# A compressed-interaction layer in pairs of chunks over two PSUM banks

## The reference

```python
# input: (512, 64, 16); W0: (128, 64*64); W1, W2: (128, 64*128)
for W, b in params:
    z = jnp.einsum('bhd,bfd->bhfd', x_vec, input)
    B, h, f, d = z.shape
    z = z.reshape(B, h * f, d)
    x_vec = jnp.einsum('oc,bcd->bod', W, z) + b[None, :, None]
    outs.append(x_vec.sum(axis=2))
return jnp.concatenate(outs, axis=1)
```

## Time and profile before

| | us |
|---|---|
| median of 3 runs | 1128.33 |
| lowest, highest | 1128.06, 1129.62 |
| the profiled execution | 1127.95 |
| its span, first to last instruction | 1126.2 |
| TensorE busy | 1095.7 |
| VectorE busy | 868.8 |
| GpSimd busy | 836.8 |
| ScalarE busy | 451.4 |

### The profile page before, as it was taken

How to read it: one execution, slowest core, us unless ns; L and a number is a source line. 1 busy time by engine, 2 the same in 40 slices (tenths; PEclk the granted TensorE clock), 3 DMA queues, 4 the chain that set the end, 5 groups by cost and what they waited for, 6 DMA issues and landing times.

```text
span 1126.2 us, 17047 instructions
## 1 busy us (share of the span) xinstructions
PE 1095.7 (97%) x4690; PEld 786.3 (70%) x4690; DVE 868.8 (77%) x3008; ACT 451.4 (40%) x1533; POOL 836.8 (74%) x765
## 2 busy tenths in 40 slices
PE   5989999999999999999999999999999999999996
PEld 5766667666677667666678666676677776666776
DVE  3556879888884888879794798978887598888990
ACT  1443435343432444434351343534343243434550
POOL 4568887969784697878875788787978479697561
PEclk9999999999999999999999999999999999999998
DMA  7952414223141231405141051423323142240000
GB/s 245 251 114 60 112 54 94 73 56 104 17 122 36 58 102 24 124 27 122 46 103 47 17 122 45 105 62 80 87 42 95 31 94 73 51 109 9 1 1 29
DMA packets 112352, 85.82 MB, mean 76 GB/s; under 512 B 75136, under 2 KB 77920, under 8 KB 112128
## 3 DMA queue, kind: packets, MB, share of 16 engines
q1 hardware_dynamic: 110528, 78.37, 28.9%
q10 hardware_dynamic: 1728, 6.36, 1.5%
HBM read 14.75 MB, written 0.79 MB: 14 GB/s over the span
## 4 chain that ended last, share of the span: by engine, by line
PE 83%; DVE 13%; issue 2%; DMA 1%; ACT 1%; POOL 1%; SPq 0%; POOLq 0%; ACTq 0%
PE y L692 53%; PE l L705 19%; DVE acc L619 8%; PE xt L755 5%; PE l2p L767 3%; DVE bd L584 2%; DVE w1l L673 1%; DVE x1l L594 1%; DMA gram<-in_L_rec_W_dram 1%; PE l2p L744 1%; DMA z<-xg 0%; PE l2p L717 0%; ACT prod L525 0%; PE xt L737 0%; PE l L727 0%
## 5 line engine op out<-in xcount | busy, mean ns | idle before, releaser
L619 DVE SCALAR_TENSOR_TENSOR acc<-y,x0t,acc 128x128 f32<-128x128 f32 x2560 | 698.8, 341 | 206.1 <-PE y L692 204.0
L525 ACT ACTIVATE prod<-y,x0t 128x128 f32<-128x128 f32 x1280 | 366.0, 369 | 610.5 <-PE y L692 578.7
L692 PE MATMUL y<-w1h,x1h 128*128 128x512 f32 x1024 | 509.3, 497 | 6.0 <-DVE acc L619 4.3
L692 PE MATMUL y<-w1h,x1l 128*128 128x512 f32 x1024 | 403.5, 394 | 0.0
L692 PE MATMUL y<-w1l,x1h 128*128 128x512 f32 x1024 | 402.4, 393 | 0.0
L371 POOL TENSOR_TENSOR pacc<-pacc,prod 128x512 f32<-128x512 f32 x192 | 247.4, 1289 | 191.6 <-ACT prod L525 191.6
L360 POOL TENSOR_TENSOR z<-z,xg 128x512 f32<-128x512 f32 (+2 forms) x272 | 348.3, 1288 | 23.7 <-DMA z<-xg 23.7
L692 PEld LDWEIGHTS y<-w1h,x1h 128*128 128x128 f32 x1024 | 192.8, 188 | 132.8 <-issue 59.2
L705 PE MATMUL l<-z,w0t 128*128 128x512 f32 (+1 forms) x512 | 257.5, 585 | 0.6 <-POOL z L360 0.6
L692 PEld LDWEIGHTS y<-w1l,x1h 128*128 128x128 f32 x1024 | 192.8, 188 | 82.2 <-issue 54.1
L692 PEld LDWEIGHTS y<-w1h,x1l 128*128 128x128 f32 x1024 | 192.1, 188 | 43.6
(11 more groups left out here) (65 smaller groups left out, 300.8 us busy)
## 6 DMA issues: line engine op xcount, KB each, us to landing
z<-xg SPq DMA_DIRECT2D x480, 128.0 KB, 2.4
xg<-in_r_input_dram SPq DMA_DIRECT2D x32, 128.0 KB, 3.9
w2t<-in_L_rec_W_dram ACTq DMA_DIRECT2D x8, 512.0 KB, 7.1
gram<-in_L_rec_W_dram SPq DMA_DIRECT2D x8, 512.0 KB, 5.9
z<-xg SPq DMA_DIRECT2D x32, 96.0 KB, 4.0
z<-xg SPq DMA_DIRECT2D x15, 192.0 KB
gram<-in_L_rec_W_dram ACTq DMA_DIRECT2D x1, 2048.0 KB, 7.9
out_dram<-z SPq DMA_DIRECT2D x4, 192.0 KB, 2.1
```

What stands on the lines that cost most here:

```text
L525: last = nc.scalar.activation(prod[:, h % HSLOTS, k, :], y[c % YB][:, k * O:(k + 1) * O], ACT.Copy, scale=x0t[:, j, f:f + 1])
L619: ins = nc.vector.scalar_tensor_tensor(out=to, in0=of, scalar=x0t[:, j, f:f + 1], in1=b1r[:] if m == 0 else to, op0=ALU.mult, op1=ALU.add)
L692: ins = nc.tensor.matmul(to, stationary, moving, start=(first and k == 0), stop=(last and k == 2))
```

## The change

`chunk` is replaced by `two_chunks`, which runs at even c for the chunks c and c + 1. The wait for the bank is split off as `bank_free`. For each of the two chunks it waits for the bank and does the two passes with x1h; then come the two passes with x1l, each of which completes a chunk and raises `y_made`. So x1h is the stationary operand of four passes in a row and x1l of two, and two banks are open at once. The number of passes and the arithmetic per bank are as before, and the other engines' lists are the same.

```diff
-            def chunk(tile, j, c):
+            def bank_free(tile, c):
 
                 before, late = (c - YB) % CHUNKS, c < YB
                 if before in HELPED:
@@ -777,9 +777,17 @@
                 else:
                     value = SN * tile + (SN + CF * SUMMED.index(before) + CF) - (SN if late else 0)
                     pe.wait_ge(acc_step, value)
+
+            def two_chunks(tile, j, c):
+
                 cols = slice(j * P, (j + 1) * P)
-                by_parts(y[c % YB][:], x1h[:, cols], x1l[:, cols], w1h[:, c, :], w1l[:, c, :],
-                         True, True, True).then_inc(y_made, 1)
+                for k in (c, c + 1):
+                    bank_free(tile, k)
+                    nc.tensor.matmul(y[k % YB][:], x1h[:, cols], w1h[:, k, :], start=True, stop=False)
+                    nc.tensor.matmul(y[k % YB][:], x1h[:, cols], w1l[:, k, :], start=False, stop=False)
+                for k in (c, c + 1):
+                    nc.tensor.matmul(y[k % YB][:], x1l[:, cols], w1h[:, k, :], start=False,
+                                     stop=True).then_inc(y_made, 1)
...
-                    chunk(tile, j, c)
+                    if c % 2 == 0:
+                        two_chunks(tile, j, c)
```

## The result

The changed kernel takes 1143.64 us (median of 4, 1142.66 to 1144.25) against 1128.19 for the kernel before in the same comparison: a ratio of 1.0135, interval 1.0123 to 1.0147. It is 15.5 us slower; 1142 was forecast.

The account below looks back on a forecast made before the run. TensorE was taken to bound most of a group, VectorE a dense stretch around each group's end. 1127.95 + 11.7 + 3.0 - 1.0 = 1141.7, with 0.4 to the median 1142 us; range 1129 to 1150, about 0.8.

Parts of the forecast that it names:

- Part 1, the loads: TensorE's weight loads: 4690 as before, all hidden; steps with changed or unchanged operand give -3 to +3 us, -1 taken.
- holding pays: Rival, chance 0.12: TensorE steps keeping their operand cost 0.213 us, saving 16 us in all, so 1126.
- Part 2, the passage: Dense stretch, chunks 56 to 9' (stroke: next group): later results and bank stalls, 0.78 us per group, +11.7 us over fifteen.
- The last group: Group without layer 0, VectorE-paced: tiles go from 12.10 to 13.07 us; three remaining tiles add +3.0 us.
- What else moves: Layer-0 steps, layer-2 matmuls and W2 turns now behind odd chunks: counted as nothing, -1 to +1 us.
- The slip at 56 is absorbed: Rival, chance 0.14: the 0.42 us at chunk 56 is lost, waits at 61, 3', 7' stay; 1136.
- Nothing changes: Rival, chance 0.08: the four banks cushion everything and loads are as before; 1128.
- it spreads: Rival, chance 0.06: each of the 48 tiles with layer 0 also stalls one step, 11 us more; 1153.

Follow-up runs that it names:

- snake: Changed kernel's pairs with one bank open at a time, second chunk starting with its x1l pass so operands are still held; 1125.4 us, beside 1125.0 for moved.
- moved: Changed kernel's pairs with passes chunk by chunk, so only layer-0, layer-2 and turn work due at even chunks moves behind the odd chunk; 1125.0 us.
- own_moved: moved, with bd for a group's last tile made on VectorE after chunk 50 instead of 59; 1115.3 us.

## Why the prediction was right, and where it was off

- **Part 1, the loads: right, but its -1 us was not there.** 4690 loads, all behind passes but those held back by a wait; `snake` shows that holding gives nothing (1125.4 to 1125.0), so the term is 0. The rival "holding pays" is out. The rule of the Trainium skill that I set against the trace (TensorE: Matmul & The Clock Gate, section The mechanism) fails again: the changed kernel and `snake` load the same rows behind streaming passes and keep 0.23 a step.
- **Part 2, the passage: right in place and size.** Stalls forecast at 61, 0', 3', 4', 7' as 0.44, 0.58, 0.17, 0.11, 0.33; measured 0.45, 0.47, 0.16, 0.12, 0.33. The shift of VectorE's chain was 0.47 for 0.42. Against the kernel before, a group got 0.69 longer for the forecast 0.78, and 0.81 longer against `moved`: the 0.11 of the moved work lies between. The two halves, tried alone, and VectorE's load, taken away, show the mechanism and not only its sum.
- **The last group: right in kind, small by a fifth.** Tiles 13.27 apart for 13.07, so the term of 3.0 us was nearer 3.9 (from chunk 56 of the fifteenth group to the end of VectorE's work +4.6, less 0.7 for the passage). VectorE waits at 8 and 14 as said: by the distance of starts 2, 6, 8 and 14 come 0.11, 0.12, 0.35 and 0.35 late, for 0.1, 0.1, 0.35 and 0.45. The missing 0.2 is bd: from chunk 11's first operation to chunk 12's are 1.99 us for 1.76, with bd itself at 1.03 instead of 0.81. It is longer because it starts earlier within GpSimd's addition and ends 0.29 and 0.28 us after it; first before, then after the change:

```profile
1070.26 1.27 POOL L371 TENSOR_TENSOR pacc<-pacc,prod 128x512 f32<-128x512 f32 x1 [0.76 <-ACT prod L525]
1071.01 0.81 DVE L584 TENSOR_TENSOR bd<-x0t,own_half 128x256 f32<-128x256 f32 x1
```

```profile
1083.04 1.28 POOL L371 TENSOR_TENSOR pacc<-pacc,prod 128x512 f32<-128x512 f32 x1 [1.23 <-ACT prod L525]
1083.57 1.03 DVE L584 TENSOR_TENSOR bd<-x0t,own_half 128x256 f32<-128x256 f32 x1
```

- **"What else moves": wrong.** I held it for nothing and named only W2's turns. The move gives about 2.5 us (`moved`, less what lies before the first layer-1 pass). In the changed kernel the first group keeps 0.4 of its 0.85, and a wait that I did not see takes some 1.4 back: chunk 28 of the long groups, behind ScalarE's copy of the quarter. Some 0.6 us of gain are left. The step that failed is the sentence that what moved "needs nothing sooner and its readers have a tile's slack": true of the moved instructions, but the late result of chunk 26 holds ScalarE, and something else was queued there. W2's turns did as said: two waits left of four, 2.0 us in the changed kernel.
- **The rivals.** "The slip at 56 is absorbed" is out: VectorE begins 56 after a wait of 0.17 for its result. "Nothing changes" and "it spreads" are out: in groups with layer 0 no chunk stalls outside the dense stretch and chunk 28 in the changed kernel.

The forecast was 13.7 us on top of the profiled execution before; the profiled executions are 16.3 apart. The 2.6 are +1.0 for the saving taken in Part 1, +0.9 in the last group, +0.4 in the passages (15 x 0.81 against `moved`, for 11.7), -0.6 for the moved work and +0.9 of tail. The medians are only 15.5 apart, since the profiled execution lies 0.2 under its kernel's median before and 0.6 above it after. So the passage, by far the largest term, was sized well, and what is missing is made of small terms; the gain of the moved work, which I had not counted, hides 0.6 of it.

## To carry to other kernels

Interleaving two accumulations delays the first result and needs the second bank sooner. Where the reader of the banks was the bound, the cost went by the sum of both slips: 0.23 us for one step, 0.45 for two, 0.8 for three a passage, whichever way the three were split. With the reader's load halved these waits were gone. Away from it, the late result cost 0.5 us a time where other work was queued behind its reader (chunk 28). So look for the stretches in which the reader has no idle time rather than at its share of the span: here they are a quarter of each group, while the span shows 77%. The same view pointed to the gain: one VectorE operation of 1.03 us carried out of that stretch brought 10 us in the plain order (at its new place it takes 0.41).

## What the runs showed of the hardware

- The order of stationary operands had no price: steps that keep it and steps that change it, to the same bank or to another, all average 227 to 233 ns by kind for 512 fp32r columns at the full clock, and the means of the thirteen kernels are 229.6 to 230.9.
- A first pass whose load had to wait for its bank makes the second start 0.39 us after the release at 61, 3', 4' and 7' (519.02, 524.65 and 527.87 above are 0.33 after their first passes), so 0.10 more than a step from the first pass on. I take this for the load, which was held back too; no run parts it from another cause. That the late load is for the operand already in place (61, 3', 7') does not shorten it against 4', where it is not.
- Making bd, one operation with both operands in SBUF, took VectorE between 0.41 and 1.43 us before and 0.57 to 1.54 after, for the same 128x256 operands. The traces show what it goes with: in the 13 kept traces, 832 makings, it either takes 0.41 to 0.42 us or ends 0.27 to 0.29 us after the end of a GpSimd operation that was at work when it started. The rows with the last group above are two of the second kind; here is one of the first, from `own_moved`, where GpSimd's operation ends as bd begins:

```profile
500.28 0.74 POOL L379 TENSOR_TENSOR pacc<-pacc 128x256 f32<-128x256 f32 x1
501.02 0.41 DVE L584 TENSOR_TENSOR bd<-x0t,own_half 128x256 f32<-128x256 f32 x1
```

So a change of order on TensorE can lengthen a VectorE operation by moving it against GpSimd's. No run changes GpSimd's work alone, so the waiting is read from the ends and not tried.
